# An audio tower with a mixture of experts on one core: two experts' weights instead of four loaded after the base store, and behind three gathers

## The chip, the cores and the metric

The kernel runs on one core of one Trainium2 chip. The core has five engines that run side by side: TensorE (PE, matrix products), VectorE (DVE), ScalarE (ACT), GpSimd (POOL) and SyncE (SP). SyncE here issues DMAs and counts what has landed; ACT and POOL issue DMAs too. All of these transfers run on the core's 16 DMA engines. The metric is the time of one execution on the device, in microseconds (us); lower is better.

## The reference

The input is 64 clips. Each is cut into 15 tokens, so there are 960 tokens of 192 numbers. A linear embedding is followed by attention within each clip (over a layer norm, with a residual), and then by a mixture of experts with 16 experts, of which each token takes its best 4:

```python
h = _L0_tok_ref(x, L0_tok_W, L0_tok_b)                      # 64 x 15 x 192
h = h + _L0_attn_ref(_layernorm(h), L0_attn_W_qkv, ...)
h = h + _L0_ffn_ref(_layernorm(h), ...)
...
t = rmsnorm(x, norm_scale)                                  # inside _L0_ffn_ref
g = jnp.einsum('bth,eh->bte', t, gate_w) + gate_b
top_vals, top_idx = jax.lax.top_k(g, K)                     # K = 4 of E = 16
route_w = jax.nn.softmax(top_vals, axis=-1)
h = jnp.einsum('nh,ech->nec', t_flat, mlp1_w) + mlp1_b      # 192 -> 2 x 384
a = swiglu(h)
y = jnp.einsum('nec,ehc->neh', a, mlp2_w) + mlp2_b          # 384 -> 192
return x + jnp.einsum('neh,ne->nh', y, comb).reshape(B, T, H)
```

## The kernel before

The 960 tokens are 8 tiles of 120. The first stage embeds them tile by tile, runs the attention and the gate, and ACT stores each tile's normalised rows into a table `t_rows` in device memory (`store_t`, L549), and at last the combine weights of all tokens beside them (L572). Then tables are made: the 3,840 pairs of token and expert are sorted by expert into 45 tiles of 128 slots (`MT`). `get_row` names the token row of each slot, `put_row` the output row, and `owner` the expert of each tile, in rising order. The last product of the tables is L1067, and VectorE copies it to `get_row` (L832), `pad_now` and `put_row` (L834, L836) and makes two small tables for the scatters (L840, L845).

The expert stage then runs over the 45 tiles. For tile j, POOL gathers 128 rows of `t_rows` by an indirect DMA (L465), TensorE turns them (`turn_x`, L1080), ACT copies the result to `xT` (L594), and ACT and VectorE each copy half of the expert's first weights to `stage` (`stage_half`, L611 and L858). TensorE makes the two up-products (L1098) and the down-product (L1107). ACT scales the result (L619), and POOL adds it to the output rows by another indirect DMA (the scatter, L481). Three gathers are issued ahead, a fourth behind them (`GATHERS` is 4); POOL issues them in order with the scatters. The first gather waits for `get_row` and for all 9 stores into `t_rows`. The first scatter waits for the base store, which puts the residual and the second bias, `h`, into the output (L352).

The order of the weights is written out on SyncE's queue. SyncE loads the first inputs, then the token tiles with one expert behind each from the fourth on, and then the remaining experts. An expert is two DMAs (`load_expert`, L326 and L327) into a place of its own, 96 x 1536 and 128 x 576 four-byte numbers. Ahead of expert 12 (`E - HELD`) SyncE waits for the last addition to `h` (L828, `s_b2c`), issues the base store, and goes on with experts 12 to 15. When all of this is issued it counts the landed experts in order: for each it waits for the expert's semaphore and adds 1 to `s_ready` (L357, L358).

TensorE's `here(j)` (L1086) reads the owner of tile j and waits until `s_ready` is above it; from tile 12 (`SETTLED`) it waits for all 16. It then adds 1 to `s_here` (L1090), and ACT and VectorE wait for that before they stage tile j.

Of the kernel before, what the change touches and what calls it, by code (L numbers as in the profile page):

```python
# [21 lines left out]
TOKENS = CLIPS * SEQ  # L22
TILES = 8
TT = TOKENS // TILES
# [6 lines left out]
E, K, I = 16, 4, 384  # L31
# [13 lines left out]
RING = 3  # L45
GATHERS = 4
GROUP = 4
SETTLED = 12
HELD = 4
FIRST = (0, 2, 6, FC)  # L50
EARLY = TILES - 2
POOL_EVERY = 3
# [2 lines left out]
def audio_tower_kernel(nc, x, tok_w, tok_b, qkv_w, qk_b, v_b, norm_scale, gate_w, gate_b,  # L55
                       w1, b1, w2, b2, out):
    ctx = ExitStack()
    with ctx:
        def sb(name, shape, dt=F32):
            return ctx.enter_context(nc.sbuf_tensor(name, shape, dt))  # L60

        def sem(name):
            return ctx.enter_context(nc.semaphore(name))
# [33 lines left out]
        h = sb("h", [TT, TILES, H])  # L97
# [117 lines left out]
        s_w = [sem(f"s_w{e}") for e in range(E)]  # L215
        s_ready = sem("s_ready")
# [55 lines left out]
        s_b2c = sem("s_b2c")  # L272
# [18 lines left out]
        s_got = [sem(f"s_got{c}") for c in range(GATHERS)]  # L291
        s_put = [sem(f"s_put{c}") for c in range(RING)]
        s_base_out = sem("s_base_out")
# [15 lines left out]
        def owners(engine, g):  # L309

            n = min(GROUP, MT - GROUP * g)
            _, found = nc.values_load_multi_w_load_instructions(
                owner[0:1, GROUP * g:GROUP * g + n], engines=[engine], min_val=0, max_val=E - 1,
                skip_runtime_bounds_check_because="owner is a count of 0 or more, held to E - 1")
            return found
# [3 lines left out]
        @block.sync  # L319
        def _(sp):  # L320
            for n in range(len(FIRST) - 1):
                c = slice(FIRST[n], FIRST[n + 1])
                sp.dma_start(tokw_sb[:, c, :], tok_w[:, c, :]).then_inc(s_first[n], 16)
                sp.dma_start(x_ring[:, 0, c], x[0][:, c, :]).then_inc(s_first[n], 16)
            def load_expert(e):
                sp.dma_start(w1_sb[0:HK, e * W1E:(e + 1) * W1E], w1[e]).then_inc(s_w[e], 16)  # L326
                sp.dma_start(w2_sb[:, e * W2E:(e + 1) * W2E], w2[e]).then_inc(s_w[e], 16)  # L327

            sp.dma_start(tokb_sb[:, :], tok_b.broadcast_to([TT, H])).then_inc(s_tokb, 16)
            sp.dma_start(qkvw_sb[:, :, 0:3 * H + 1], qkv_w).then_inc(s_qkvw, 16)  # L330
            sp.dma_start(qkb_sb[:, :], qk_b).then_inc(s_qkvw, 16)
            sp.dma_start(vb_sb[:, :], v_b.broadcast_to([TT, H])).then_inc(s_small, 16)
            for i in range(1, TILES):
                if i >= RING:
                    sp.wait_ge(s_emb, i - RING + 1)
                sp.dma_start(x_ring[:, i % RING], x[i]).then_inc(s_x[i % RING], 16)
                if i == 1:
                    sp.dma_start(nscale_sb[:, :], norm_scale.broadcast_to([TT, H])).then_inc(s_small, 16)
                    sp.dma_start(gateb_sb[:, :], gate_b.broadcast_to([TT, E])).then_inc(s_small, 16)
                    sp.dma_start(gatew_sb[:, :, :], gate_w).then_inc(s_small, 16)  # L340
                    sp.dma_start(b2_sb[:, :], b2).then_inc(s_small, 16)
                if i == RING:
                    sp.dma_start(w1_sb[HK:HK + 1, :].rearrange("p (e c n) -> p e c n", e=E, c=HC)[:, :, HC - 1, :],
                                 b1).then_inc(s_b1, 16)

                if i > RING:
                    load_expert(i - RING - 1)
            for e in range(TILES - RING - 1, E):
                if e == E - HELD:

                    sp.wait_ge(s_b2c, 4)
                    sp.dma_start(out[0:TOKENS, :].rearrange("(i p) n -> p i n", p=TT), h[:, :, :]).then_inc(s_base_out, 16)  # L352
                load_expert(e)


            for e in range(E):
                sp.wait_ge(s_w[e], 32)  # L357
                sp.sem_inc(s_ready, 1)  # L358

            sp.wait_ge(s_base_out, 16)  # L360
            for c in range(RING):
                sp.wait_ge(s_put[c], 16 * len(range(c, MT, RING)))
# [815 lines left out]
```

## Time and profile before

| what | us |
|---|---|
| three runs | 289.96, 290.88, 291.25; median 290.88 |
| the profiled execution | 291.94 |
| its span, first to last instruction | 290.2 |
| TensorE busy within the span | 256.5 |
| POOL, VectorE, ACT busy | 172.6, 168.7, 113.3 |

The profile is of one execution. Its views used here are: the waits (who waited for whom), the chain of work that ended last (followed back from the last instruction), the stretches (busy time by engine in a window, with the granted clock of TensorE and the share and rate of the DMA engines), and the order of instructions in time. Times count from the start of the span. A DMA's row shows how long its issue took; its flight, from issue to landing, stands in the views of DMAs. Some 1.7 us of the profiled execution lie outside the span.

### The profile page before, as it was taken

The numbers are of one execution on the slowest core, as the hardware profiler recorded it, in microseconds if no ns is written. First come the engines' busy times: TensorE is split into PE (matmuls) and PEld (weight loads), VectorE is DVE, ScalarE is ACT, GpSimd is POOL, SyncE is SP. The second block draws the span as 40 slices with busy tenths as digits, with TensorE's granted clock in tenths as the row PEclk, the third lists the DMA queues.
The fourth block names the chain that finished last, engine by engine and source line by source line (L and its number), as shares of the span: only waits on it lengthen the run. The fifth ranks groups of instructions, "written<-read, shape, count | busy, mean of one in ns | idle before, by whom it ended". The sixth has DMA issues, their size and how long they took to land.

```text
span 290.2 us, 6337 instructions
## 1 busy us (share of the span) xinstructions
PE 256.5 (88%) x1943; PEld 249.8 (86%) x1943; DVE 168.7 (58%) x425; ACT 113.3 (39%) x291; POOL 172.6 (59%) x202
## 2 busy tenths in 40 slices
PE   2899999997577079999999999999999999999980
PEld 1799999986456079999999999999999999999970
DVE  0014465567897117676676766767766667676640
ACT  1010212233142125545554555455455545554520
POOL 5013266668897412567776666767766666665752
PEclk9999999999655559999999999999999999999996
DMA  6998999999812993323423243422322333233100
GB/s 180 232 216 201 235 229 232 270 278 282 241 16 58 259 244 105 48 34 56 62 49 47 45 58 54 59 42 31 50 47 49 51 49 56 32 43 52 19 1 0
DMA packets 18589, 31.29 MB, mean 108 GB/s; under 512 B 5629, under 2 KB 12125, under 8 KB 18557
## 3 DMA queue, kind: packets, MB, share of 16 engines
q1 hardware_dynamic: 7862, 22.33, 31.2%
q0 software_dynamic: 8640, 7.76, 17.6%
q10 hardware_dynamic: 2055, 0.80, 1.1%
q8 instruction: 16, 0.26, 0.4%
q14 instruction: 16, 0.13, 0.1%
HBM read 26.39 MB, written 5.96 MB: 111 GB/s over the span
## 4 chain that ended last, share of the span: by engine, by line
PE 78%; DMA 9%; POOL 5%; issue 2%; DVE 2%; POOLq 1%; SPq 1%; ACT 1%; DVEq 0%
PE bank L1098 39%; PE bank L1107 14%; PE bank L905 11%; DMA hn_all<-t_rows,get_row 4%; PE bank L1080 3%; DMA x_sb<-in_x 3%; PE bank L1048 2%; PE bank L934 2%; PE bank L942 2%; DMA out<-hn_all,put_row 2%; PE bank L951 1%; POOL ln_all L429 1%; PE bank L914 1%; PE bank L1067 1%; POOL rstd L422 1%
## 5 line engine op out<-in xcount | busy, mean ns | idle before, releaser
L1098 PE MATMUL bank<-xT,x_sb 96*128 96x128 f32 (+1 forms) x1080 | 136.9, 276 | 0.8 <-ACT xT L594 0.8
L1098 PEld LDWEIGHTS bank<-xT,x_sb 96*128 96x128 f32 (+1 forms) x1080 | 131.6, 193 | 1.2 <-issue 1.2
L481 POOL DMA_INDIRECT out<-hn_all,put_row x45 | 73.0, 1622 | 52.5 <-issue 23.2
L465 POOL DMA_INDIRECT hn_all<-t_rows,get_row x45 | 47.2, 1049 | 21.0 <-issue 12.5
L1107 PE MATMUL bank<-w_sb,tokw 128*128 x270 | 51.4, 326 | 0.7 <-DVE tokw L880 0.7
L1107 PEld LDWEIGHTS bank<-w_sb,tokw 128*128 128x128 f32 x270 | 42.9, 190 | 1.0 <-issue 1.0
L869 DVE TENSOR_SCALAR ln_all<-bank 128x384 f32<-128x384 f32 x45 | 25.1, 558 | 31.4 <-PE bank L1098 31.4
L905 PE MATMUL bank<-tokw,x_sb 120*120 120x192 f32 x192 | 37.0, 353 | 6.8 <-DMA x_sb<-in_x 6.8
L611 ACT COPY x_sb<-w_sb 96x768 f32 x45 | 37.0, 823 | 12.4 <-PEq L1090 10.3
L905 PEld LDWEIGHTS bank<-tokw,x_sb 120*120 120x120 f32 x192 | 34.2, 199 | 7.8 <-DMA x_sb<-in_x 7.8
L873 DVE TENSOR_TENSOR ln_all<-ln_all 128x384 f32<-128x384 f32 x45 | 25.2, 560 | 26.5 <-ACT ln_all L630 26.5
L619 ACT ACTIVATE hn_all<-bank,weight 128x192 f32<-128x192 f32 x45 | 19.0, 421 | 49.6 <-PE bank L1107 49.6
L630 ACT ACTIVATE ln_all<-ln_all 128x384 f32<-128x384 f32 x45 | 23.5, 523 | 36.7 <-DVE ln_all L869 36.7
L858 DVE COPY x_sb<-w_sb 97x768 f32 x45 | 25.7, 573 | 6.3 <-PEq L1090 5.6
L1080 PE MATMUL bank<-ident,hn_all 128*96 128x128 f32 x90 | 17.8, 280 | 10.1 <-DMA hn_all<-t_rows,get_row 10.1
L880 DVE SCALAR_TENSOR_TENSOR tokw<-ln_all 128x384 f32<-128x384 f32 x45 | 25.2, 561 | 1.6
L875 DVE TENSOR_SCALAR ln_all<-bank 128x384 f32<-128x384 f32 x45 | 24.8, 551 | 1.2 <-PE bank L1098 1.1
L1080 PEld LDWEIGHTS bank<-ident,hn_all 128*96 128x96 f32 x90 | 10.7, 130 | 10.7 <-issue 9.8
L409 POOL TENSOR_TENSOR var_eps<-mv,eps_sb 120x1 f32<-120x1 f32 x8 | 1.8, 231 | 26.9 <-DVE mv L665 26.9
L662 DVE TENSOR_TENSOR h<-bank,tokb_sb 120x192 f32<-120x192 f32 x8 | 2.9, 358 | 25.7 <-PE bank L905 25.7
L594 ACT COPY xT<-bank 96x256 f32<-96x256 f32 x45 | 15.8, 351 | 2.7 <-PE bank L1080 2.7
L532 ACT COPY probT<-bank 120x120 f32<-120x120 f32 x8 | 2.1, 259 | 19.3 <-PE bank L959 19.3
(143 smaller groups left out, 229.4 us busy)
## 6 DMA issues: line engine op xcount, KB each, us to landing
w_sb<-in_w SPq DMA_DIRECT2D x16, 576.0 KB, 14.8
x_sb<-in_x SPq DMA_DIRECT2D x7, 675.0 KB, 10.9
w_sb<-in_w SPq DMA_DIRECT2D x16, 288.0 KB, 15.9
t_rows<-hn_all ACTq DMA_DIRECT2D x8, 90.0 KB, 7.9
out<-h SPq DMA_DIRECT2D x1, 720.0 KB, 6.1
hn_all<-t_rows,get_row POOLq DMA_INDIRECT x45, 3.2
out<-hn_all,put_row POOLq DMA_INDIRECT x45, 3.5
tokw<-in_tok_w SPq DMA_DIRECT2D x1, 540.0 KB, 6.7
```

What stands on the lines that cost most here:

```text
L465: g.indirect_dma_start(out=xg[slot], out_offset=None, in_=t_rows, in_offset=bass.IndirectOffsetOnAxis(ap=get_row[:, m:m + 1], axis=0),).th ...
L481: g.indirect_dma_start(out=out, out_offset=bass.IndirectOffsetOnAxis(ap=put_row[:, m:m + 1], axis=0), in_=ysb[m % RING], in_offset=None, c ...
L611: a.copy(stage[0:HK, j % 2, 0, :], w1_sb[0:HK, bass.ds(experts[j] * W1E, 2 * I)]).then_inc(s_stage_0, 1)
L858: d.tensor_copy(stage[:, j % 2, 1, :], w1_sb[0:HK + 1, bass.ds(experts[j] * W1E + 2 * I, 2 * I)]).then_inc(s_stage_1, 1)
L869: d.tensor_scalar(glu, ps_glu, LIMIT, None, ALU.min).then_inc(s_gluc, 1)
L873: d.tensor_tensor(gs, glu, sig, ALU.mult).then_inc(s_gs, 1)
L875: d.tensor_scalar(lin, ps_lin, LIMIT, -LIMIT, ALU.min, ALU.max).then_inc(s_linc, 1)
L880: d.scalar_tensor_tensor(out=aT[:, j % 2], in0=lin, scalar=1.0, in1=gs, op0=ALU.add, op1=ALU.mult).then_inc(s_a, 1)
L905: ins = t.matmul(ps_emb[i], x_ring[:, i % RING, c, :], tokw_sb[:, c, :], start=(c == 0), stop=(c == FC - 1))
L1080: ins = t.transpose(ps_xT[:, c, :], xg[j % GATHERS][:, c * HK:(c + 1) * HK], ident[:, :])
L1098: ins = t.matmul(dst[:, m * SLOTS:(m + 1) * SLOTS], stage[0:rows, j % 2, c, o:o + 128], xT[0:rows, j % 2, c, :], start=(c == 0), stop=(c = ...
L1107: ins = t.matmul(ps_y, aT[:, j % 2, c * SLOTS:(c + 1) * SLOTS], w2_sb[:, bass.ds(experts[j] * W2E + c * H, H)], start=(c == 0), stop=(c == ...
```

## The change

`HELD` becomes 2, so experts 0 to 13 are issued without a wait. SyncE then counts these 14 as they land, waits for the last addition to `h`, and issues the base store. Then it waits for the first three gathers (`GATHERS - 1`, semaphores `s_got[0]` to `s_got[2]`), issues experts 14 and 15, and counts them.

```diff
-HELD = 4
+HELD = 2
...
-            for e in range(TILES - RING - 1, E):
-                if e == E - HELD:
-
-                    sp.wait_ge(s_b2c, 4)
-                    sp.dma_start(out[0:TOKENS, :].rearrange("(i p) n -> p i n", p=TT), h[:, :, :]).then_inc(s_base_out, 16)
+            for e in range(TILES - RING - 1, E - HELD):
                 load_expert(e)
 
 
-            for e in range(E):
+            for e in range(E - HELD):
+                sp.wait_ge(s_w[e], 32)
+                sp.sem_inc(s_ready, 1)
+
+
+            sp.wait_ge(s_b2c, 4)
+            sp.dma_start(out[0:TOKENS, :].rearrange("(i p) n -> p i n", p=TT), h[:, :, :]).then_inc(s_base_out, 16)
+            for m in range(GATHERS - 1):
+                sp.wait_ge(s_got[m], 16)
+            for e in range(E - HELD, E):
+                load_expert(e)
+            for e in range(E - HELD, E):
                 sp.wait_ge(s_w[e], 32)
                 sp.sem_inc(s_ready, 1)
```

## Rows read from the trace of the kernel before

**Rows 1.** The head of the profile's page: span and instructions.
```profile
span 290.2 us, 6337 instructions
```

**Rows 2.** Waits before 105 us, and TensorE's after 104: total, times, longest.
```profile
PE bank L1080 <- DMA hn_all<-t_rows,get_row: 9.6, 1, 9.6
...
PE bank L1080 <- DMA hn_all<-t_rows,get_row: 0.4, 1, 0.4
```

**Rows 3.** Chain that ended last, 88 to 115 us: start, length, what.
```profile
90.23 2.53 PE bank L1067 x32
...
93.30 8.95 DMA hn_all<-t_rows,get_row
...
102.38 0.65 PE bank L1080 x2
...
103.84 2.90 PE bank L1098 x12
...
110.66 1.34 PE bank L1098 x12
...
114.53 0.56 PE bank L1098 x5
```

**Rows 4.** Stretches: length, busy PE, PEld, DVE, ACT, POOL; clock, DMA share, GB/s.
```profile
74.14:80.00 5.86, 3.93 (x26) 3.44 (x26) 5.23 (x23) 0.86 (x3) 5.53 (x9) 0.50 0.81 237
80.00:92.00 12.00, 9.89 (x54) 7.84 (x54) 10.45 (x38) 5.30 (x12) 10.83 (x18) 0.50 0.07 9
92.00:96.00 4.00, 0.75 (x10) 0.55 (x8) 1.16 (x7) 0.00 (x0) 2.21 (x2) 0.50 0.94 211
96.00:102.30 6.30, 0.00 (x0) 0.00 (x0) 1.03 (x2) 0.83 (x1) 1.89 (x2) 0.50 1.03 256
103.80:108.30 4.50, 4.46 (x21) 4.46 (x22) 0.93 (x2) 1.31 (x4) 0.94 (x1) 0.50 1.04 245
108.30:112.50 4.20, 4.20 (x38) 4.20 (x38) 2.93 (x7) 1.71 (x4) 0.00 (x0) 1.00 0.81 208
```

**Rows 5.** SyncE's queue in time: start, length, line, DMA issued.
```profile
91.10 0.37 SPq L352 DMA_DIRECT2D out<-h  x1
...
98.10 0.55 SPq L327 DMA_DIRECT2D w_sb<-in_w  x1
```

**Rows 6.** DMA issues: count, KB each, median us to landing.
```profile
t_rows<-hn_all ACTq DMA_DIRECT2D x8, 90.0 KB, 7.9
out<-h SPq DMA_DIRECT2D x1, 720.0 KB, 6.1
...
t_rows<-comb ACTq DMA_DIRECT2D x1, 60.0 KB, 2.3
```

**Rows 7.** The gathers' line: ns to issue, min/median/max; and their landing.
```profile
L465 POOL DMA_INDIRECT hn_all<-t_rows,get_row x45: 944/988/1491, 93.3 to 270.3; - x45
...
DMA to landing us min/median/max: 2.6/3.2/8.8
```

**Rows 8.** Instructions in time, ACT and VectorE, around the first staging.
```profile
82.64 0.34 ACTq L572 DMA_DIRECT2D t_rows<-comb  x1
...
93.71 0.30 DVE L845 SCALAR_TENSOR_TENSOR x_sb<-x_sb 1x44 int32<-1x44 int32 x2
...
99.55 0.83 ACT L611 COPY x_sb<-w_sb 96x768 f32 x1 [10.30 <-PEq L1090]
99.59 1.03 DVE L858 COPY x_sb<-w_sb 97x768 f32 x2 [5.57 <-PEq L1090]
```

**Rows 9.** The first gather; the scatter's line; one scatter and VectorE's copy within.
```profile
93.30 1.26 POOL L465 DMA_INDIRECT hn_all<-t_rows,get_row  x1 [1.95 <-DVE get_row L832]
...
L481 POOL DMA_INDIRECT out<-hn_all,put_row x45: 1552/1588/2118, 114.4 to 283.5; - x45
...
259.00 2.12 POOL L481 DMA_INDIRECT out<-hn_all,put_row  x1 [0.36 <-issue]
260.48 0.56 DVE L858 COPY x_sb<-w_sb 97x768 f32 x1
```

## The prediction

> **What bounds the kernel now.** I read four views, from the whole down to the place that the change touches.
>
> The waits first, and TensorE's own. The core's span is 290.2 us [rows 1]. Before the expert stage begins TensorE waits 9.6 us for one thing, the landing of the first gather, and after 104 us it waits 0.4 us for gathers in all the rest of the run [rows 2]. So one long stall stands in front of the expert stage, and behind it the stage is TensorE's.
>
> The chain of waits around 90 to 115 us gives the order. The product that makes the tables (L1067) starts at 90.23, the first gather is issued at 93.30 and counts 8.95 us, so it lands at 102.25; the transposition begins at 102.38 and the first expert product at 103.84, 1.59 us after the landing [rows 3]. The tiles that follow start 3.87 us apart (110.66 to 114.53), back to back on TensorE [rows 3]. A shift of the first product is therefore a shift of the end, unless something else is late.
>
> Then the stretches, for the DMA engines. From 74.14 to 80 they are 0.81 busy; from 80 to 92 they are 0.07 busy at 9 GB/s, that is idle for some 11 us; from 92 to 102.3, the very time in which the gather flies, they are 0.94 and 1.03 busy at 211 and 256 GB/s [rows 4]. SyncE's queue says with what: the base store goes out at 91.10 and the last of the four experts is issued at 98.10 [rows 5]. A gather takes 3.2 us at the median from issue to landing and 2.6 at least; the worst took 8.8 [rows 7], and the first is that long one. So the gather is slow because 720 KB of store and four experts of 864 KB go through the same engines, while the 11 idle us just before were given away.
>
> **The change part by part.**
>
> Two experts move ahead of the base store. An expert is 576 KB and 288 KB by the slices of `load_expert`, 0.885 MB in bytes, so two are 1.77 MB. At the 237 to 256 GB/s of [rows 4] that is 6.9 to 7.5 us, appended to traffic that ends at about 80: they land by 87.0 to 87.5. The base store is issued at 91.10 because SyncE waits for the last addition of L828; it now also stands behind the landing of expert 13 (the count of 14 experts sits ahead of it on SyncE's queue). The cover is 91.1 - 87.5 = 3.6 us, so I cost this at nothing; without the cover each us would move the base store, not the gather, by one.
>
> The same traffic lies beside ACT's stores of token rows, which the first gather waits for. The last of them, the combine weights, is issued at 82.64 [rows 8] and landed 2.3 us later in an idle stretch [rows 6]. Beside expert loads such a store took 7.9 us at the median [rows 6]: 82.64 + 7.9 = 90.5, against 93.30 when the gather is issued. Cost nothing, cover 2.8 us. This is the thinnest cover in the sum.
>
> The count moves ahead. Before, the count of the landed experts begins only when SyncE has issued everything (98.10 + 0.55 = 98.65), and ACT and VectorE make their staging copies at 99.55 and 99.59 [rows 5, 8], waiting on TensorE's sequencer, which waits for the count: ACT's wait is 10.3 us [rows 8]. Those copies are done by 100.6, ahead of the gather's 102.25, so today this second gate costs nothing, but without this part it would take the gather's place. With the count long done, the gate opens when the tables' product ends (90.23 + 2.53, so 92.8) plus the same 0.9 us that passed from 98.65 to 99.55: 93.7. ACT's copy (0.83) then ends at 94.5; VectorE is busy to 94.0 with the last table (93.71 + 0.30) and its two copies (1.03 together [rows 8]) end at about 95.4. That is before the gather lands (below), so nothing of it is on the path.
>
> The last two experts wait on SyncE for the first three gathers. Behind that wait on SyncE's queue stand only those four DMAs and their two counts. Who waits for these counts: TensorE at tile 12 asks for all 16, some 10 tiles of 3.87 us after the first product; the last two land about 8 us after it. Cost nothing, cover some 30 us. Gather 4, issued after the first product has begun, still flies beside these two experts as it did beside four; TensorE wants it four tiles later.
>
> The stall. What is left beside the gather in its flight is the base store. The first gather is issued at 93.30 as before, since neither the tables nor POOL's order change. Bounds of its landing: below, the quickest gather, 93.30 + 2.6 = 95.9 [rows 7]. Above: it gets nothing until the base store has landed, 91.10 + 6.1 = 97.2 [rows 6], and then needs what a quick gather needs after its descriptors are written, 2.6 - 1.0 = 1.6: 98.8. I take the median 3.2 and add 0.27, as writing its descriptors takes 1.26 us against 0.99 at the median [rows 7, 9], and 0.3 for the store's tail and for VectorE's copies: 93.30 + 3.8 = 97.1. It is nearer to the lower end because in 92 to 96 the engines move 4.0 us x 211 GB/s = 0.84 MB, more than the whole store (0.74 MB): the store is nearly through by 96.
>
> VectorE's copies deserve a word, as they move to just where the descriptors are written. The row: a scatter's descriptors took 2.12 us from 259.00, against 1.59 at the median, and VectorE's copy L858 ran from 260.48 to 261.04 inside it, so one copy costs up to 0.53 [rows 9]. The Trainium skill, SBUF — State Buffer, section "SBUF: two separate sides", has a rule that speaks against the change here: an fp32 SBUF-to-SBUF copy of VectorE locks GpSimd out of the port by which it writes descriptors, so the transfer stands still. The trace agrees by that 0.53 us; by the rule in full, both copies would hold up the first gather, which is the first rival below with its 286.5 us, against 285.7 by the row.
>
> **The sum.** Landing 102.25 becomes 97.1: -5.15, say -5.2 us for the first product (103.84 to about 98.65). The expert stage behind it is costed as a pure shift, POOL's loop included, since its scatters follow TensorE's results. The clock: TensorE is granted 0.50 from 74.14 on (1.2 GHz) and gets 1.00 (2.4 GHz) at 108.3, 4.5 us after the first product [rows 4]. I let this rise move with the product. Counted from the transposition at 102.38 it is 5.9; the difference of 1.4 us at half speed is worth 0.7 us, either way. The profiled execution took 291.94 us around its span of 290.2 and would take 286.7; the runs' median of 290.88 (289.96 to 291.25) becomes 285.7.
>
> **The rivals.**
>
> *Descriptors starve.* Both copies of VectorE fall into the first gather's descriptor writing: 2 x 0.53 = 1.06 us in place of the 0.3 I took, so 0.8 more. For it: the copies can start at about 94.3, and the writing lasts to 94.56 at least. Against: by then most of the descriptors are written, and the second copy would hit gather 1, which TensorE wants 2.7 us later. 286.5 us. Chance 0.10.
>
> *The clock does not follow.* The rise stays at its date, 108.3, since the stretch 80 to 92 shows 9.89 us of busy TensorE at 0.50 without a rise [rows 4]. Then half speed lasts from 98.65 to 108.3, 9.65 us in place of 4.5, and 5.15 / 2 = 2.6 us go back: 288.3. Against: those matmuls are small ones, and the rise did follow the dense products. Chance 0.04.
>
> *The experts were not the cause.* The first gather is slow for itself or for the base store, and lands at 102.25 again; the change then does not do what it is for: 290.9. For it: the store goes out at the same 91.10. Against: engines that stay 1.03 busy till 102.3, when the store has landed at 97.2 [rows 4, 6]. Chance 0.06.
>
> *A table store late (slower).* The combine weights' store, issued at 82.64, is stuck behind experts 12 and 13, and the gather waits for it. It costs one us for each us that it lands after 93.30, and makes the kernel slower once it lands after 98.5, that is 15.9 us after its issue. If it took 20 us, the gather would be issued at 102.6 and land at 106.4, 4.2 us late: 295.1. Against: ACT's stores beside full traffic took 7.9 at the median, and the traffic ends at about 87.5. Chance 0.03.
>
> **How the numbers follow.** The forecast, 285.7, has the remaining 0.77. Its own range: landing at 95.9 is a gain of 6.35, and 0.7 more from the clock, 283.8; landing at 98.8 is a gain of 3.45, less 0.7, 288.1. That takes in the first rival, and I leave the others out: 283.8 to 288.1. Half a per cent, 1.45 us, is about what a measurement can tell here from no change. Faster: 0.77 + 0.10 + 0.04 = 0.91; same 0.06; slower 0.03.
>
> **What would show it.** Right: the first gather's flight near 3.8 us; TensorE's wait for it near 4.3 instead of 9.6; DMA engines busy from 80 to about 87 and idle until the base store, still at 91.1; ACT's first staging copy at about 93.7 to 94; the last two experts issued at about 99 to 100; tiles 3.87 us apart. Wrong: the base store after 91.1, a first gather issued after 93.3, staging copies that end after the gather lands, a clock that rises more than 6 us after the first product, or new waits of TensorE for gathers among the tiles.

## The result: 1.4% faster, and the gather gained more than the run

The changed kernel took 287.24 us at the median of 20 runs against 291.32 for the kernel before (20 runs beside it). The ratio is 0.986 (0.984 to 0.988), a gain of 4.2 us with 3.5 to 4.8 as its interval. Measured twice more beside other kernels it came to 0.990 (0.986 to 0.993) and 0.982 (0.978 to 0.987). Ratios leave out the executions that took over 1.5% longer than the fastest of their kernel; medians keep them. The forecast was 5.2 us. The profiled execution took 287.27 us around a span of 285.5, against 291.94 around 290.2.

The chain of waits of the changed kernel from 85 to 115 us (start, length, what), where [rows 3] stood before; seven lines of code more move L1098 to L1105 and L1080 to L1087:

```profile
93.24 3.26 DMA hn_all<-t_rows,get_row
...
96.64 0.65 PE bank L1087 x2
...
98.08 2.90 PE bank L1105 x12
...
101.41 4.26 PE bank L1105 x24
...
105.89 1.34 PE bank L1105 x12
...
109.77 1.34 PE bank L1105 x12
```

The first gather is issued at 93.24 instead of 93.30 and lands at 96.50 instead of 102.25. The first expert product starts at 98.08 instead of 103.84, 5.76 us earlier. The tile that started at 110.66 starts at 105.89, though: only 4.77 earlier. From there to the end of the span both kernels need 179.6 us (290.2 - 110.66 = 179.5; 285.5 - 105.89 = 179.6), so the rest is a pure shift. (The clock falls again near the end, at 285.8 and 278.7, but behind TensorE's last product, which ends at 282.3 and 277.6.) The missing 1.0 us lies between the first product and 105.89, where nothing waits; the two up-products at 101.41 simply take 4.26.

The stretches show why (length, busy PE, PEld, DVE, ACT, POOL; clock, DMA share, GB/s), to be read against [rows 4]:

```profile
74.14:80.00 5.86, 4.00 (x26) 3.44 (x26) 5.24 (x23) 0.80 (x3) 5.53 (x9) 0.50 1.04 287
80.00:92.00 12.00, 9.89 (x54) 7.92 (x54) 10.39 (x38) 5.29 (x12) 10.77 (x18) 0.50 0.67 157
...
102.30:106.00 3.70, 3.70 (x25) 3.70 (x25) 2.30 (x5) 1.02 (x3) 0.00 (x0) 0.69 1.00 287
106.00:110.00 4.00, 4.00 (x36) 4.00 (x35) 2.74 (x6) 2.01 (x5) 0.36 (x1) 1.00 0.21 59
```

The once idle stretch from 80 to 92 now moves 157 GB/s in place of 9: the two experts. The mean clock of 0.69 from 102.3 to 106 is a rise from 0.50 to 1.00 with (0.69 - 0.50) / 0.50 x 3.7 = 1.4 us at full speed, so the rise came at 104.6, 6.5 us after the first product. In the kernel before it came at 108.3, 4.5 us after. Two more microseconds at 1.2 GHz cost one. The clock fell at about the same time in both, 74.1 and 73.9, so the stretch at 1.2 GHz shrank from 34.1 to 30.7 us: by 3.4, where the stall shrank by 5.7.

SyncE's queue, the DMA issues (median us from issue to landing), ACT's first staging copy, and the second gather beside VectorE's first two staging copies:

```profile
91.04 0.37 SPq L358 DMA_DIRECT2D out<-h  x1
98.89 0.32 SPq L326 DMA_DIRECT2D w_sb<-in_w  x1
...
100.19 0.43 SPq L327 DMA_DIRECT2D w_sb<-in_w  x1
```

```profile
t_rows<-hn_all ACTq DMA_DIRECT2D x8, 90.0 KB, 8.2
out<-h SPq DMA_DIRECT2D x1, 720.0 KB, 5.0
...
t_rows<-comb ACTq DMA_DIRECT2D x1, 60.0 KB, 7.3
```

```profile
94.10 0.83 ACT L618 COPY x_sb<-w_sb 96x768 f32 x1 [4.92 <-issue]
94.80 0.96 POOL L472 DMA_INDIRECT hn_all<-t_rows,get_row  x1 [0.30 <-issue]
...
95.00 1.14 DVE L865 COPY x_sb<-w_sb 97x768 f32 x2 [1.05 <-issue]
```

The base store still goes out at 91.04, and ACT stages at 94.10 instead of 99.55. The combine weights' store now takes 7.3 us instead of 2.3 and lands at about 90, 3 us ahead of the first gather's issue. The last DMA of the experts ahead, issued at 64.52 and 24.8 us in flight, lands at 89.3.

### The profile page after: what moved, and what is told of

Same layout as the page of the kernel before. It is cut to its first block, busy times and chain, and to the rows that moved or that the text cites. A ratio compares the mean times of both kernels' runs of the same rounds, so it can differ in the third digit from the quotient of the medians.

```text
span 285.5 us, 6338 instructions
## 1 busy us (share of the span) xinstructions
PE 257.6 (90%) x1943; PEld 250.8 (88%) x1943; DVE 169.2 (59%) x425; ACT 113.1 (40%) x291; POOL 173.0 (61%) x202
## 4 chain that ended last, share of the span: by engine, by line
PE 79%; DMA 7%; POOL 5%; issue 3%; DVE 2%; POOLq 1%; ACT 1%; SPq 1%; ACTq 0%; DVEq 0%
PE bank L1105 39%; PE bank L1114 14%; PE bank L912 11%; PE bank L1087 3%; DMA x_sb<-in_x 3%; DMA hn_all<-t_rows,get_row 2%; PE bank L1055 2%; PE bank L941 2%; PE bank L949 2%; DMA out<-hn_all,put_row 2%; PE bank L958 1%; POOL ln_all L436 1%; PE bank L921 1%; PE bank L1074 1%; POOL rstd L429 1%
## 5 line engine op out<-in xcount | busy, mean ns | idle before, releaser
L1105 PE MATMUL bank<-xT,x_sb 96*128 96x128 f32 (+1 forms) x1080 | 137.9, 278 | 0.8 <-ACT xT L601 0.8
L1105 PEld LDWEIGHTS bank<-xT,x_sb 96*128 96x128 f32 (+1 forms) x1080 | 132.6, 195 | 1.2 <-issue 1.2
L865 DVE COPY x_sb<-w_sb 97x768 f32 x45 | 26.4, 588 | 1.8 <-issue 1.6
L882 DVE TENSOR_SCALAR ln_all<-bank 128x384 f32<-128x384 f32 x45 | 24.8, 551 | 1.9 <-PE bank L1105 1.9
L1087 PE MATMUL bank<-ident,hn_all 128*96 128x128 f32 x90 | 17.9, 281 | 4.4 <-DMA hn_all<-t_rows,get_row 4.3
L1087 PEld LDWEIGHTS bank<-ident,hn_all 128*96 128x96 f32 x90 | 10.7, 130 | 5.1 <-issue 4.1
```

The source lines that it names most:

```text
L865: d.tensor_copy(stage[:, j % 2, 1, :], w1_sb[0:HK + 1, bass.ds(experts[j] * W1E + 2 * I, 2 * I)]).then_inc(s_stage_1, 1)
L882: d.tensor_scalar(lin, ps_lin, LIMIT, -LIMIT, ALU.min, ALU.max).then_inc(s_linc, 1)
L1087: ins = t.transpose(ps_xT[:, c, :], xg[j % GATHERS][:, c * HK:(c + 1) * HK], ident[:, :])
L1105: ins = t.matmul(dst[:, m * SLOTS:(m + 1) * SLOTS], stage[0:rows, j % 2, c, o:o + 128], xT[0:rows, j % 2, c, :], start=(c == 0), stop=(c = ...
```

## The experiments

All are compared with the kernel before on the same chip. The changed kernel's own ratio, where it ran in the same set, stands beside them.

**Each part by itself.** The first set takes the change apart: the early count, the wait for the gathers, and the number of experts held.

The count put back behind all issues:

```diff
-            for e in range(E - HELD):
-                sp.wait_ge(s_w[e], 32)
-                sp.sem_inc(s_ready, 1)
...
-            for e in range(E - HELD, E):
+            for e in range(E):
```

> The changed kernel, but SyncE counts all 16 experts only behind its last issue, as before the change. Theory (the count is a second gate for the first product, hidden before behind the slow gather): SyncE has issued everything at about 100.6, staging copies start 0.9 us later at 101.5, the first product starts at about 102.5 instead of 98.08, though the first gather still lands at about 96.5. About 4.4 us later: 291.6 us against 287.2, no gain left over the kernel before. Rival (the count is bookkeeping, only the gather's flight matters): 287.2.

The ratio is 1.002 (0.996 to 1.007): all of the gain is gone. TensorE's waits, and two pieces of the chain:

```profile
PE bank L1082 <- SPq L360: 9.1, 1, 9.1
```

```profile
101.82 0.65 PE bank L1082 x2
...
103.29 2.90 PE bank L1100 x12
```

TensorE's wait before the first transposition is nearly as long as in the kernel before (9.1 us against 9.6), but its releaser is now SyncE's count and no longer the gather. ACT stages at 101.46, as expected, but the first product starts at 103.29, 0.8 later than I expected: on TensorE's queue the transposition stands behind the waits for the count as well, so it starts only at 101.82, and the 1.47 us from there to the first product follow. I had looked at the staging alone. So the gather's gain comes through only with the early count, which by itself is worth nothing: the next kernel has the early count too.

The wait for the gathers taken out, so that two experts follow the base store at once:

```diff
-            for m in range(GATHERS - 1):
-                sp.wait_ge(s_got[m], 16)
```

> The changed kernel without SyncE's wait for the three gathers: two experts are sent right behind the base store, the count of 14 stays ahead. Theory (a gather crawls as long as any expert streams beside it): store and two experts are 2.5 MB, at 211 to 256 GB/s from 92 us on they end at about 102, and the first gather lands at 100 to 102, so 290.7 to 292.5 us. Rival (only the amount beside it counts, two are half of four): landing at about 99, 289.7 us. Second rival (moving two experts ahead and the count is the whole gain, the wait is idle): 287.2 us.

The ratio is 1.003 (0.998 to 1.007). The chain:

```profile
92.23 8.41 DMA hn_all<-t_rows,get_row
...
102.25 2.90 PE bank L1103 x12
```

The gather's flight is 8.41 us beside two experts, against 8.95 beside four [rows 3] and 3.26 beside the base store alone. The time and the landing, 100.64, came as the theory had them, and both rivals fell. Its wording does not fit the kernel before, though: there the gather landed at 102.25, while the engines were still 0.81 busy from 108.3 to 112.5 [rows 4], some 10 us later. So a gather does not wait for the stream's end. Common to both flights is that the engines are full all the way through, and then it took 8.4 to 9 us, with two experts or four. ACT's stores of token rows paid about the same in the kernel before, 7.9 us at the median [rows 6], beside a stream whose expert loads, issued from 40 to 60 us, took 22.2 and 24.8.

Four experts held back, with wait and early count (`HELD = 4`):

> The changed kernel with four experts held back instead of two: the wait for the gathers and the early count without moving any expert ahead of the store. Theory (the gain is that nothing streams beside the gathers): the first gather lands at 96.5 as with two held, 287.2 us within 0.7. The combine weights land 2.3 us after their issue instead of 7.3, which gives nothing, since the gather waits for its table until 93.2 either way. Rival (the two experts moved ahead carry half of the gain): about 289 us.

The ratio is 0.994 (0.989 to 0.9995), about half of the gain or less. The times alone do not quite tell it from the changed kernel, whose second measurement reached 0.993; the profile does. It is the rival's time, by a way that I had not named. The gather lands at 96.40 and the first product starts at 97.98, as in the changed kernel. TensorE's waits for gathers add up to 7.5 us, though, against 4.3 in the changed kernel. Here are those waits (total, times, longest), a stretch, and POOL's scatters and gathers in time, all with four held:

```profile
PE bank L1087 <- DMA hn_all<-t_rows,get_row: 7.5, 4, 4.3
```

```profile
112.00:114.00 2.00, 2.00 (x21) 2.00 (x19) 0.91 (x2) 1.38 (x3) 0.00 (x0) 1.00 1.00 241
```

```profile
109.03 1.64 POOL L488 DMA_INDIRECT out<-hn_all,put_row  x1 [9.68 <-ACT hn_all L626]
110.98 1.00 POOL L472 DMA_INDIRECT hn_all<-t_rows,get_row  x1 [0.30 <-issue]
115.91 1.65 POOL L488 DMA_INDIRECT out<-hn_all,put_row  x1 [3.93 <-ACT hn_all L626]
```

and with two held:

```profile
PE bank L1087 <- DMA hn_all<-t_rows,get_row: 4.3, 2, 4.0
```

```profile
109.64 1.64 POOL L488 DMA_INDIRECT out<-hn_all,put_row  x1 [10.13 <-ACT hn_all L626]
111.58 1.00 POOL L472 DMA_INDIRECT hn_all<-t_rows,get_row  x1 [0.31 <-issue]
114.00 1.59 POOL L488 DMA_INDIRECT out<-hn_all,put_row  x1 [1.42 <-DMA out<-hn_all,put_row]
```

With four held the experts stream until 114, and the first scatter, issued at 109.03, flies among them. The second scatter waits for the first one's landing (the profile names ACT, whose result for it had long been there) and is issued at 115.91 instead of 114.00, though its tile came earlier. The gathers stand behind the scatters in POOL's order, so later ones are late, and TensorE waits 1.4 us at 122 and 1.1 at 135. With two held the DMA engines are 0.21 busy from 106 to 110 (above), so the experts have landed at about 107, before the first scatter. That is what moving two of them ahead of the store is worth.

No expert held back (`HELD = 0`):

> The changed kernel with no expert held back: all 16 go ahead of the base store, none behind. Theory (the idle stretch before the store holds two experts, not four): the experts' traffic ends at about 94.5 to 95 instead of 87.7, the combine weights land after 93 and hold the first gather back, the base store moves to about 95 and flies beside the gather; landing at 99 to 100.5, first product at 100.5 to 102, 289.7 to 291.2 us. Rival (only what streams behind the store hurts): 287.2 us.

The ratio is 1.004 (0.997 to 1.011). The chain:

```profile
82.38 14.83 DMA t_rows<-comb
...
98.12 5.02 DMA hn_all<-t_rows,get_row
...
104.75 2.90 PE bank L1105 x12
```

This is the forecast's slower rival, carried out, though the ratio shows only that the gain is gone and not a loss: the combine weights' store, 60 KB, takes 14.8 us beside four experts, and the gather, released by it and no longer by its table, is issued at 98.12 instead of 93.24. The first product starts 3 us later than I expected. The base store was issued at 97.10, behind the last expert's landing, and the gather beside it flew 5.0 us.

**The covers, and what is left in the gather's flight.** The second set was run beside the changed kernel again.

> The changed kernel itself, unaltered, beside the three below on one chip: 0.986 of the kernel before if the gain is the kernel's and not the chip's. It also gives a second date for the rise of TensorE's clock: in the first profile it came 6.5 us after the first product of the expert stage, in the kernel before 4.5; in four other kernels 3.7 to 5.9. Theory (the delay varies by execution): anywhere from 3.7 to 6.5 us. Rival (the change makes it longer): 6.5 again.

The ratio is 0.990 (0.986 to 0.993). The rise of the clock came 6.7 us after the first product (97.71 to 104.4), beyond the theory's range and near the rival's 6.5.

One expert held back (`HELD = 1`):

> The changed kernel with one expert held back instead of two: the cover of the combine weights' store and of the base store, taken away by 3.5 us. The combine weights took 2.3 us with no expert beside, 7.3 with two, 14.8 with four. Theory: about 11 with three, landing at 93.5 to 94, which holds the first gather back by 0.3 to 0.8 us; the base store goes out at about 91.5 instead of 91.04 and flies a little longer beside it. 287.5 to 288.5 us. Rival (the cover is only thin, not gone): 287.2.

The ratio is 0.988 (0.982 to 0.994), not to be told from the changed kernel. The combine weights' store took 9.3 us, less than the 11 that I had put between 7.3 and 14.8, so it landed at about 91.7, and the cover was thin but not gone. The base store went out at 91.31 and the gather's flight was 3.89 us; the first product came at 98.49, 0.4 to 0.8 later, as expected in size, but by the base store alone. The execution with a profile ended no later, since its clock rose 5.4 us after the product.

The base store issued behind the wait for the gathers:

```diff
-            sp.wait_ge(s_b2c, 4)
-            sp.dma_start(out[0:TOKENS, :]...)
             for m in range(GATHERS - 1):
                 sp.wait_ge(s_got[m], 16)
+            sp.wait_ge(s_b2c, 4)
+            sp.dma_start(out[0:TOKENS, :]...)
```

> The changed kernel with the base store issued behind the wait for the three gathers instead of ahead of it, so that nothing streams beside the first gather. Theory (what is left in the gather's flight is the store, and it costs at most 3.26 - 2.6 us): the gather lands at 95.9 to 96.5, and the two experts, behind the store now, end at about 109.5 instead of 106.6, at the first scatter's issue (109.6), so nothing comes of it behind: 286.6 to 287.2 us. Rival (the experts now touch the first scatter, and POOL falls behind as with four held back, 115.91 instead of 114.00 for its second scatter, and TensorE waits for gathers 6 and 9): 288 to 289 us.

The ratio is 0.990 (0.985 to 0.994), again the changed kernel's time. The gather's flight, and TensorE's waits for gathers:

```profile
93.70 2.99 DMA hn_all<-t_rows,get_row
```

```profile
PE bank L1087 <- DMA hn_all<-t_rows,get_row: 5.0, 2, 3.7
```

The flight was 2.99 us, 0.2 to 0.3 shorter, so the store's price in it is some 0.3 us by this one profile. The rival's way occurred beside it: the second scatter came 5.6 us after the first one instead of 4.4, POOL fell behind, and TensorE waited 1.4 us for a gather at 133. In this execution the clock's rise at 102.0, 2.1 to 2.6 us earlier than in the changed kernel, made up for most of that. So the equal time does not show that nothing came of it.

**The clock.** The gain is short of the gather's by 1 us, and the clock's late rise is the only thing in the profile that accounts for it. If the rise followed dense products, filler products in TensorE's idle stretch would bring it forward. In four kernels I put such products, of 96 x 128 by 128 from expert 0's weights into a bank that nobody reads.

```diff
             pe.wait_ge(s_b2c, 1)
+            pe.wait_ge(s_owner, 2)
+            pe.wait_ge(s_w[0], 32)
+            for n in range(14):
+                t.matmul(bank[7][0:128, 0:128], w1_sb[0:HK, 0:128], w1_sb[0:HK, 128:256], start=True, stop=True)
             turn_x(0)
```

> The changed kernel with 14 dense products of 96 x 128 by 128 on TensorE, into a bank that nobody reads, in the idle stretch before the first transposition. They add work and change no result. Theory (the clock's rise follows dense products, and half speed at the start of the expert stage costs half of its length): the products run at half clock from about 92.8 to 96.2, the rise comes 3.7 to 6.5 us after 92.8, at 96.5 to 99.3, instead of 104.6, so 0.5 to 2.8 us of half speed are left behind the first product instead of 6.5; 2 to 3 us faster than the changed kernel, about 284.7 us. Rival (the clock has its own date and does not follow): no gain, 287.2, or a loss of up to 0.5 where the products overrun the landing.

The ratio is 0.988 (0.984 to 0.993), beside the changed kernel's 0.990. The chain, and a stretch:

```profile
94.18 6.32 PE bank L1125 x28
...
101.27 1.58 PE bank L1105 x12
```

```profile
98.00:102.00 4.00, 3.45 (x20) 3.22 (x20) 0.00 (x0) 1.19 (x3) 0.07 (x2) 0.70 0.68 166
```

The rise came early, at 100.4 (0.70 over 4 us), and the first product ran at full speed. But a product is two records of 0.226 us, which I had counted as one, so the filler lasted until 100.5 and held up the transposition, of a gather issued at 93.02, by some 4 us. The two cancel.

The same with 8 products right behind the last product of the tables, and the first two `here` calls ahead of that:

> The changed kernel with 8 dense products on TensorE right behind the last product of the tables, and TensorE's first two waits for the count moved ahead of that product, so that the dense products start at 92.7 and end at 96.3, before the landing, and do not hold up the staging. They add work and change no result. Theory (the clock rises 3.7 to 6.7 us after dense products begin, and the 14 products lost their gain because they began at 94.2 and overran the landing by 4 us): rise at 96.4 to 99.4, first product at 98.1, so 0 to 1.3 us at half speed instead of 5 to 6.5; 2 to 2.8 us faster than the changed kernel, 0.978 to 0.98 of the kernel before. Rival (the half clock costs little, since the tiles wait for something else): as the changed kernel, 0.986 to 0.990.

The ratio is 0.985 (0.981 to 0.989); the changed kernel did not run in this set. The tables' last product ended at 94.12 instead of 92.70, which I put down to the moved waits, and the chain has the filler from 94.12 to 97.67 and the first product at 99.17. The rise did not come forward, as this stretch shows (0.72 over 3 us, so at 104.7):

```profile
103.00:106.00 3.00, 3.00 (x22) 3.00 (x22) 1.56 (x3) 1.40 (x4) 0.00 (x0) 0.72 1.06 306
```

Dense products also in the idle places from 69 to 82.6 us:

> The kernel with 8 dense products, and further dense ones in TensorE's idle places from 69 to 82.6 us (5, 3, 6 and 8), where its clock falls at about 74. They add work and change no result. Theory A (the clock falls for want of dense products and stays at full speed with them): the clock stays at 1.00 through 92.7, TensorE's chain from 82.66 to 92.7, 10 us of products at half speed today, shrinks by up to 4 us, less up to 1 us by which the dense ones hold up the others: 0.965 to 0.975 of the kernel before. Theory B (the light products of the tables let the clock fall in any case): nothing beyond the kernel with 8, or up to 1 us lost: 0.978 to 0.985.

The ratio is 0.986 (0.983 to 0.989). The clock fell at 76.1 in spite of them and the filler then ran at half speed, ahead of products on the path; the tables were ready 1.6 us later. Theory A fell. Behind the tables the filler began at 94.3, and three stretches show what the clock did then:

```profile
95.00:98.00 3.00, 2.34 (x14) 2.15 (x13) 1.58 (x7) 0.83 (x1) 2.40 (x3) 0.73 0.67 174
98.00:102.00 4.00, 2.63 (x14) 2.43 (x14) 0.00 (x0) 1.19 (x3) 2.63 (x3) 0.76 0.46 91
102.00:105.00 3.00, 3.00 (x22) 2.98 (x22) 1.54 (x3) 1.16 (x4) 0.00 (x0) 0.76 0.92 260
```

It rose at 96.6, fell again at 100.0 and rose for good at 103.4. Before the second fall TensorE had stood idle for some 1 us ahead of the transposition and 1 us ahead of the first product, at 99.77. The early rise did not last.

5 products before the transposition and 2 behind it, beside the changed kernel for a third time:

> The changed kernel with 5 dense products between TensorE's waits for the count and the first transposition, and 2 behind it while ACT copies the turned rows. They add work and change no result. One call was two records of 0.226 us at half clock, so the 14 calls lasted 6.3 us and overran the landing; the 8 calls that began at 94.1 were followed by 0.8 us of idle TensorE, and the clock rose only at 104.7. Here the dense work starts at 94.2, reaches the landing (96.4) within 0.2 us and leaves no gap of over 0.3 us before the first product at 98.1 to 98.4. Theory (the rise follows an unbroken dense stretch, wherever that begins): it comes at 98 to 101 instead of 104.4, and 1.5 to 3 us are gained over the changed kernel: 0.976 to 0.983 of the kernel before. Rival (the rise follows the expert stage's own products): 104 or later, no gain, 0.986 to 0.992.

> The changed kernel once more, beside the next one on the same chip: 0.984 to 0.993 of the kernel before, as in its two measurements. For the date of the clock's rise: Theory (in this kernel's usual run the delay is long, which takes back some 1 us of the gather's gain): 6.0 to 6.7 us after the first product, as in its first two profiles (6.5 and 6.7). Rival (chance of the execution): anywhere from 3.7 to 6.7.

The filler gave 0.989 (0.985 to 0.993), the changed kernel 0.982 (0.978 to 0.987). With the filler the rise came at 102.0, 7.4 us after the dense work began at 94.65 and between the two forecasts, and the first product started 0.5 later (98.55). In the changed kernel it came at 104.2, 6.1 us after the product at 98.01. So the rise came 2 to 4 us earlier for good in two of the four kernels with filler in that place, and no ratio gained by it.

The kernel with the store behind has no filler, and its clock rose at 102.0 too; but there it had fallen at 71.3, 2.1 to 2.6 us earlier than in the changed kernel's three profiles. The date of the fall differed from profile to profile, 71.3 to 76.1. Counted from it, the stretch at 1.2 GHz tells the kernels apart better than the rise's date does. It lasted 30.7 us in all three profiles of the changed kernel and also with one held, with four held, with the store behind and with the 8 products; 34.1 in the kernel before, with the late count and without the wait, whose first products came at 102 to 104; 37.6 with none held (104.75); 27.3 with 14 products and with 5 and 2. So in the profiles of two kernels with filler it was 3.4 us shorter. With 14 products the late transposition took that back; with 5 and 2 the profiled execution was shorter than the changed kernel's (span 283.7 against 285.0), but the ratio over nine runs was not better. Why the rise comes when it does is not settled by these runs. No version beat the changed kernel.

## Why the prediction was right, and where it was off

The time, 287.24, lies within 283.8 to 288.1, 1.5 us above the forecast of 285.7. Of these, 0.4 are the kernel before's own, whose median was 291.32 here and 290.88 in the forecast. The mechanism was the one forecast: the gather's long flight went, and the expert stage moved forward. Two terms of the sum were off in opposite directions, the gather's flight and the clock, and that they partly cancelled was luck.

- *The stall.* The gather's flight was put at 3.8 us between 2.6 and 5.5; it was 3.26, 3.18 and 3.33 in three profiles. Of this the store makes some 0.3, by the one profile with the store behind. I was 0.5 us too careful here.
- *VectorE's copies.* They began at 95.00, later than the 94.3 that I took as the earliest, and by then the first gather's descriptors were written (93.24 + 1.26 = 94.50). So the first rival did not occur, and its price was not put to the test on that gather. The second gather's descriptors took 0.96 us with a copy inside, against 0.95 for the third, so the copy did not stop them. The rule of the Trainium skill (SBUF — State Buffer, section "SBUF: two separate sides"), that such a copy locks GpSimd out of descriptor writing, did not show on this gather, and the measurement decides here. The 0.53 us that I read from one scatter with a copy inside [rows 9] is not shown to be the copy's either. In the same trace the scatter at 127.81 took 1.59 us, the median, with a copy inside (128.67 to 129.26), and the one at 274.76 took 1.93 with no such copy.
- *Two experts ahead.* Costed at nothing, with a cover of 2.8 us for the combine weights' store. It took 7.3 us where I took 7.9, and landed 3 us ahead of need. That the two figures agree is luck: 7.9 was the price of the stores of token rows, which kept to about 8 us with none held too, while the combine weights' store landed 0.2 to 0.6 us behind the last expert that was issued ahead of it, in every profile with an expert ahead. The price of losing the cover was right in kind: with none held the gather waits for that store. The experts themselves landed at 89.3, not by 87.5: I took the traffic of the kernel before to end at 80, but its last expert load, issued at 56.42 and 24.9 us in flight, landed at 81.3. So the base store's cover was 1.7 us and not 3.6, and it held.
- *The last two experts.* Costed at nothing too, and that held, but I named the wrong waiter. I looked at TensorE's count for tile 12, 30 us away. The nearest that could be hurt is the first scatter, at 109.6, about 2 us behind these experts' landing (at 107.5 by their flights); with four held it is hit, and about half of the gain is lost.
- *The count.* Without it none of the gain is left in this order, as forecast. The staging copies were expected at 93.7 to 94 and came at 94.10.
- *The clock.* This is the term that was mis-sized. I let the rise move with the first product, give or take 0.7 us. It came 6.5, 6.7 and 6.1 us after the product in three profiles, against 4.5 in the one before, which takes back 0.8 to 1.1 us; more than 6 us was among the prediction's own signs of being wrong. Counted as a whole, the stretch at half speed fell by 3.4 us (34.1 to 30.7) where the stall fell by 5.7, so 2.3 us of half speed, worth 1.2, were added to the products. The sum then reads 5.7 - 1.2 = 4.5, within the interval of 3.5 to 4.8. There is only one profile of the kernel before. The runs without a profile point the same way through their mean clock: 2 x (1 - mean clock) x span, the time at half speed, is 38.9 us over 58 runs of the kernel before and 35.9 over 34 of the changed one. That figure also counts the stretch behind the last product (4.4 and 6.8 us in the two profiles), which costs nothing, so it confirms the size only if these ends are alike on average. The rival in which the rise keeps its date fell: it moved from 108.3 to 104.6.

## What to carry to other kernels

When a small transfer that everybody waits for flies beside a large stream, look for idle stretches of the DMA engines just before it and for the first waiter behind it: the stream must fit in between, and both ends have a price (here the combine weights' store before, the first scatter behind). When a wait is taken away, look for the gate that opened just before it did; here it was a count on the queue of the engine that issued the stream, worth nothing until the stall was gone and everything after. And when a stall shrinks while the clock is at half speed, look at how much of the half-speed stretch goes with it: here 3.4 us of 5.7, and half of the rest was given back.

## What the runs showed of the hardware

The flight of the 60 KB store of combine weights against the experts sent ahead beside it: 2.3 us with none, 5.9 to 8.3 with two (ten profiles), 9.3 with three, 14.8 with four. In each of these twelve it landed 0.2 to 0.6 us behind the last of those experts. The 90 KB stores of token rows, on the same queue of ACT, took 8.0 to 8.7 us beside the same stream, in the changed kernel's first profile and with none held alike. The first gather: 8.95 us beside four experts, 8.41 beside two, 3.2 to 3.3 beside the base store alone in the changed kernel's three profiles, 2.99 with the store behind it. So beside full engines a gather or a store of token rows was slowed to 8 or 9 us, with two experts queued beside it or four, and the combine weights' store came through only with the stream's end. The latter writes 960 rows of 64 bytes, a store of token rows 120 of 768; whether that is the reason no run here tests. A store of token rows even passed older loads: issued at 54.52 in the changed kernel it landed at 63.1, while an expert load issued at 49.08 landed at 73.1.

TensorE's clock rose 3.7 to 6.7 us after the first product of the expert stage in the kernels without filler. Filler of the same density began 6.2, 7.4 and 10.5 us before the rise in three kernels, and 2.3 us before a rise that did not last in the fourth. Counted from the clock's fall, the stretch at 1.2 GHz was the same 30.7 us in all three profiles of the changed kernel. What decides the date stays open.
